# Linear attention in a graph layer: one product for numerators and denominators, divided with nodes on partitions, the quotient turned

## The chip, the cores and the metric

One core of one Trainium2 chip runs the whole program. The metric is the device time of one execution in microseconds. The engines are TensorE (PE, with its weight loads as PEld), VectorE (DVE), ScalarE (ACT), GpSimd (POOL) and SyncE (SP, which only issues transfers here). Each has its own stream of instructions, works it off in order, and waits for the others by semaphores.

## The reference

A layer over 6250 nodes of 256 features: layer norm, then the sum of a graph attention over 100000 edges (sorted by source node), a linear attention with feed-forward part, and a mixture of six experts. What this study touches is the linear attention:

```
q_phi = _phi(q); k_phi = _phi(k)                # (1, 6250, 8 heads, 32)
kv = jnp.einsum('blhd,blhe->bhde', k_phi, v)    # 8 heads x 32 x 32
k_sum = k_phi.sum(axis=1)
z = 1.0 / (jnp.einsum('blhd,bhd->blh', q_phi, k_sum) + 1e-06)
out = jnp.einsum('blhd,bhde,blh->blhe', q_phi, kv, z)
out = out.reshape(Bq, Lq, D_MODEL) @ Wo + bo
x = _layernorm(x + out, ln1_g, ln1_b)
```

## The kernel before, in words

The nodes are worked on in 25 chunks of 250 (two tiles of R = 125 nodes). For each chunk `c` the attention has ten or so steps on three engines. They have no time of their own: they are laid between the steps of another job, the sorting of the edges into tiles. That job is one long sequence of **slots**. Each engine runs through all slots in order, and at each slot `s` calls `attend(s)`, which runs the step with offset `d` for the chunk with `s = 6c + d` (`chunk_at`; SLOT = 6, so a new chunk begins every six slots, and a step with offset 11 runs in the slots 5, 11, 17 ... of its engine). The steps and offsets before the change:

- offset 3, PE `q`: queries with features on partitions, 128x250 per half (L1182)
- offset 4, ACT `attend_q`: exp and relu of them (L1045, L1047); offset 6, ACT `prepare` (L1038), DVE `phi` (L744)
- offset 7, PE `numden`: denominators with nodes on partitions, eight columns from `ks8` (L1191), and numerators with features on partitions from the block diagonal `kv_bd` (L1193)
- offset 8, DVE `invert`: add 1e-6 and invert, 125x16 (L749, L751); ACT `numerators`: copy of them to `att` (L1053)
- offset 9, ACT `inverses`: each inverse is written out 32 times to `rec_row` (L1058)
- offset 10, PE `inverses`: four products with the identity bring them to features on partitions (L1200)
- offset 11, DVE `divide`: `att` times the inverses (L756)
- offset 12, PE `o`: output projection and bias (L1211, L1213)
- offset 13, DVE `attend_sum` and the moments (L762, L285, L290); 14, ACT `root` (L296, L298); 15, DVE `attend_norm` (L770); 16, ACT `normal` (L1065)

The slots fall in three stretches. **Slots 0 to 49**: one masked copy of 128x784 on DVE per slot (L795) and one mask on ACT (L1093); PE has nothing but attention. **Slots 50 to 57** lie between small steps on DVE that make tables. **From slot 58** on a pass `k` (30 of them) has four slots. DVE makes in it the one-hot operands of run `k`: `first_half` (L904), slot, `low_half` (L907), slot, `payload` (L910, L911), slot, `join` (L919), slot. PE multiplies in it those of run `k-1`: slot, 7 products (`compact` part 0, L1238), slot, 7, slot, 7, slot, 7. The two are tied:

```
def first_half(k):
    if k >= 2:
        dve.wait_ge(gathered_up, k - 1)
...
    if part == 0:
        pe.wait_ge(spread_out, k + 1)
```

So DVE can't begin pass `k` before PE has ended pass `k-1`, and in pass `k` PE needs what DVE made in pass `k-1`. Slot 58 is 10 modulo 12; the attention's slots therefore fall on the passes in a pattern of three passes, which take two chunks: slots 10, 11, 0, 1 (modulo 12) in the first kind of pass, 2, 3, 4, 5 in the second, 6, 7, 8, 9 in the third.

Of the kernel before, what the change touches and what calls it, by code (L numbers as in the profile page):

```python
# [13 lines left out]
F32 = mybir.dt.float32  # L14
# [9 lines left out]
R = 125  # L24
# [103 lines left out]
def gps_kernel(nc, x, src, dst, gW, gWb, ga, gab, Wq, bq, Wk, bk, Wv, bv, Wo, bo, W1, b1, W2, b2,  # L128
# [7 lines left out]
    with ExitStack() as ctx:  # L136
# [6 lines left out]
        bank = [ctx.enter_context(nc.psum_tensor(f"bank{i}", [128, 512], F32)) for i in range(8)]  # L143
# [69 lines left out]
        kv_bd = take(2, 128)  # L213
        ks8 = take(2, 8)
# [10 lines left out]
        rec_row = take(2, 8, HD)  # L225
# [113 lines left out]
        QB, HEADS, NUM, DEN, OUT = 1, 2, 3, 4, 5  # L339
# [53 lines left out]
        m_inv = sem("m_inv")  # L393
# [47 lines left out]
        with nc.Block() as block:  # L441
# [128 lines left out]
            def _(dve):  # L570
# [162 lines left out]
                step(V.memset(ks8, 0.0))  # L733
                for h in range(2):
                    V.tensor_tensor(kv_bd[:, h, :], bank[KV + h][:, 0:128], diag_mask, ALU.mult)
                    last_i = V.tensor_scalar(ks8[:, h, 4 * h:4 * h + 4], diag_mask.rearrange("p (h e) -> p h e", h=4)[:, :, 0],
                                             bank[KV + h][:, 128:129], None, ALU.mult)
# [8 lines left out]
                def invert(c):  # L746
                    dve.wait_ge(m_nd, at(c, 1, 1))
                    wait(dve, m_rec, at(c))
                    V.tensor_scalar(den8[0:R, :, :], bank[HEADS][0:R, 0:16].rearrange("p (r h) -> p r h", r=2), 1e-6, None, ALU.add).then_inc(m_den, 1)  # L749
                    dve.wait_ge(m_den, at(c, 2, 1))  # L750
                    V.reciprocal(rec8[0:R, :, :], den8[0:R, :, :]).then_inc(m_den, 1)  # L751

                def divide(c):
                    dve.wait_ge(m_rec, at(c, 1, 1))
                    dve.wait_ge(m_num, at(c, 1, 1))
                    V.tensor_tensor(att, att, bank[DEN][:, 0:2 * CH].rearrange("p (m n) -> p m n", m=2), ALU.mult).then_inc(m_att, 1)  # L756
# [15 lines left out]
                def attend(slot):  # L772

                    c = chunk_at(slot, 15)
                    if c is not None:
                        attend_norm(c)
                    c = chunk_at(slot, 13)
                    if c is not None:
                        attend_sum(c, at(c) % 2)
                    c = chunk_at(slot, 11)  # L780
                    if c is not None:
                        divide(c)
                    c = chunk_at(slot, 8)
                    if c is not None:
                        invert(c)
                    c = chunk_at(slot, 6)
                    if c is not None:
                        phi(c)
# [166 lines left out]
            def _(act):  # L955
# [112 lines left out]
                def attend(slot):  # L1068

                    c = chunk_at(slot, 16)  # L1070
                    if c is not None:
                        normal(c, at(c) % 2)
                    c = chunk_at(slot, 14)
# [3 lines left out]
                    if c is not None:  # L1077
                        inverses(c)
                    c = chunk_at(slot, 8)
                    if c is not None:  # L1080
                        numerators(c)
# [31 lines left out]
            def _(pe):  # L1113
# [72 lines left out]
                def numden(c):  # L1186
                    pe.wait_ge(m_phi, at(c, 1, 1))
                    wait(pe, m_att, at(c))
                    for r in range(2):
                        for m in range(2):  # L1190
                            T.matmul(bank[HEADS][0:R, 8 * r:8 * r + 8], phiq[:, m, r * R:(r + 1) * R], ks8[:, m, :], start=(m == 0), stop=(m == 1))  # L1191
                    for m in range(2):
                        last = T.matmul(bank[NUM][:, m * CH:(m + 1) * CH], kv_bd[:, m, :], phiq[:, m, :], start=True, stop=True)  # L1193
                    last.then_inc(m_nd, 1)

                def inverses(c):
                    pe.wait_ge(m_inv, at(c, 1, 1))
                    for m in range(2):
                        for r in range(2):
                            last = T.matmul(bank[DEN][:, m * CH + r * R:m * CH + (r + 1) * R],  # L1200
                                            rec_row[0:R, r, 4 * m:4 * m + 4, :].rearrange("p h e -> p (h e)"), ident[0:R, 0:R], start=True, stop=True)
                    last.then_inc(m_rec, 1)

                def o(c):
                    if at(c) == 0:
                        pe.wait_ge(consts, 4)
                    pe.wait_ge(m_att, at(c, 1, 1))
# [8 lines left out]
                def attend(slot):  # L1216

                    c = chunk_at(slot, 12)
                    if c is not None:
                        o(c)  # L1220
                    c = chunk_at(slot, 10)
                    if c is not None:
                        inverses(c)
# [1158 lines left out]
```

## Time and profile before

| | |
|---|---|
| median of 3 runs | 2300.26 us (2300.15 to 2304.06) |
| profiled execution | 2298.15 us, its span 2296.4 us |
| busy share of the span | PE 83%, PEld 67%, DVE 74%, ACT 64%, POOL 49% |
| mean granted clock of TensorE | 0.926 of full speed |
| DVE's masked copies (slots 0 to 49) | begin at 329.0 us and 409.3 us |
| passes of four slots | first L904 at 450.5 us, last at 676.5 us |

A span is the time from the first instruction to the last. Busy shares are means over stages with different limits; the attention touched here lives between about 336 and 670 us, and what a step costs has to be read there. In the rows, "idle before" in brackets is how long the engine had stood still, and which engine and line ended the wait. The full clock of TensorE is 2.4 GHz, and a granted clock of 0.50 is 1.2 GHz.

### The profile page before, as it was taken

How to read it: one execution, taken by the hardware profiler on the slowest of the kernel's cores; microseconds unless marked ns; L12 is line 12 of the kernel's file. 1: busy time of each engine (PE TensorE's matmuls, PEld its weight loads, DVE VectorE, ACT ScalarE, POOL GpSimd, SP SyncE). 2: the span in 40 equal slices, each digit the busy share in tenths (PEclk: the TensorE clock that was granted, in tenths of full speed). 3: DMA queues.
4: the chain of work that ended last, by engine and by line, in shares of the span. 5: the costliest groups of instructions: out<-in, count | busy, mean ns of one | idle time of the engine just before them, and what ended most of it. 6: DMA issues, size and time to landing. Idle time of an engine off the chain costs nothing. (4 is left out here: it accounts for less than half of the span.)

```text
span 2296.4 us, 50185 instructions
## 1 busy us (share of the span) xinstructions
PE 1901.7 (83%) x10177; PEld 1538.0 (67%) x10177; DVE 1709.2 (74%) x5357; ACT 1463.3 (64%) x4497; POOL 1119.3 (49%) x1107
## 2 busy tenths in 40 slices
PE   1588858699983999999999999999998572699996
PEld 0345436488872877778777788787787462588885
DVE  7687878878884888898888888988888552255543
ACT  3566739334422888899888898988988660233332
POOL 2000000011125777777777766777774277255554
PEclk9799979699995999999999999999999665799998
DMA  4312201021113444444444444444442543255553
GB/s 137 87 50 59 59 23 50 27 76 46 44 27 83 122 117 119 121 119 120 117 118 121 114 110 115 120 116 118 117 122 71 178 161 132 65 93 91 94 97 54
DMA packets 132951, 218.68 MB, mean 95 GB/s; under 512 B 41572, under 2 KB 87135, under 8 KB 132655
## 3 DMA queue, kind: packets, MB, share of 16 engines
q0 software_dynamic: 61648, 135.33, 24.5%
q1 hardware_dynamic: 66345, 72.68, 10.6%
q10 hardware_dynamic: 4662, 7.46, 1.1%
q8 instruction: 95, 1.56, 0.3%
q14 instruction: 201, 1.65, 0.2%
HBM read 153.08 MB, written 56.42 MB: 91 GB/s over the span
## 5 line engine op out<-in xcount | busy, mean ns | idle before, releaser
L1362 POOL DMA_INDIRECT area<-wh_table,area x812 | 784.2, 966 | 275.5 <-issue 242.3
L1689 PE MATMUL bank<-area 128*126 x2008 | 495.8, 389 | 41.3 <-ACT area L1602 20.8
L1689 PEld LDWEIGHTS bank<-area 128*126 128x126 f32 x2008 | 358.0, 188 | 116.6 <-issue 67.5
L1395 DVE TENSOR_SCALAR area<-iota_row,area 128x126 f32<-128x126 f32 x1004 | 358.9, 365 | 21.2 <-ACT area L1562 15.4
L1595 ACT ACTIVATE area<-iota_row,area 128x126 f32<-128x126 f32 x753 | 292.9, 389 | 0.0
L2180 POOL DMA_INDIRECT out_dram<-area x108 | 169.6, 1571 | 163.4 <-DVE area L2241 146.6
L1609 ACT ACTIVATE area<-area 128x126 f32<-128x126 f32 x753 | 242.8, 386 | 0.5
L1548 ACT ACTIVATE area<-bank 125x512 bf16<-125x512 f32 x251 | 149.0, 594 | 85.4 <-DVE area L1409 82.3
L1470 DVE SCALAR_TENSOR_TENSOR acc_mem<-acc_mem,area,bank 125x258 f32 x251 | 120.6, 480 | 100.3 <-PE bank L1677 84.1
L1709 PE MATMUL bank<-area 128*128 128x250 f32 x800 | 188.6, 379 | 6.2 <-ACT area L1616 3.5
L1665 PE MATMUL bank<-ident,area 128*126 128x128 f32 x1004 | 162.0, 284 | 33.9 <-DVE area L1395 33.8
L1720 PE MATMUL bank<-area 128*125 128x256 f32 x800 | 189.6, 380 | 0.0
L559 POOL IOTA acc_mem<- 50x812 f32 x1 | 0.8, 807 | 353.5 <-DVE area L828 353.5
L1409 DVE TENSOR_REDUCE area<-bank 125x1 f32<-125x512 f32 x251 | 171.4, 683 | 0.0
L1709 PEld LDWEIGHTS bank<-area 128*128 128x128 f32 x800 | 153.1, 192 | 26.6 <-ACT area L1616 3.9
L1720 PEld LDWEIGHTS bank<-area 128*125 128x125 f32 x800 | 150.4, 188 | 23.7
L2241 DVE SCALAR_TENSOR_TENSOR area<-bank,area 128x256 f32<-128x256 f32 x108 | 47.3, 480 | 143.3 <-PE bank L2338 77.4
L564 POOL DMA_INDIRECT sorted_slots<-area x28 | 46.0, 1641 | 216.5 <-DVE area L919 203.4
L2273 ACT ACTIVATE area<-bank,area 128x256 f32<-128x256 f32 x108 | 45.3, 471 | 139.8 <-issue 133.6
L1665 PEld LDWEIGHTS bank<-ident,area 128*126 128x126 f32 x1004 | 106.5, 141 | 39.1 <-DVE area L1395 38.7
L1880 POOL DMA_INDIRECT moe_rows<-area x100 | 99.7, 997 | 66.8 <-ACT area L2030 37.0
L1562 ACT ACTIVATE area<-area,iota_blk 128x4 f32 x251 | 74.8, 298 | 54.8 <-SPq L1354 32.4
(416 smaller groups left out, 4147.8 us busy)
## 6 DMA issues: line engine op xcount, KB each, us to landing
area<-moe_rows SPq DMA_DIRECT2D x54, 264.0 KB, 2.7
area<-wh_table,area POOLq DMA_INDIRECT x812
area<-area SPq DMA_DIRECT2D x18, 388.5 KB
wh_table<-area SPq DMA_DIRECT2D x50, 126.5 KB
xn<-in_x_dram SPq DMA_DIRECT2D x25, 250.0 KB
xt_rows<-area SPq DMA_DIRECT2D x50, 125.0 KB, 2.4
area<-xt_rows SPq DMA_DIRECT2D x25, 250.0 KB, 2.6
x_rows<-area SPq DMA_DIRECT2D x25, 250.0 KB
```

The costliest lines, as they stand in the source:

```text
L1362: g.indirect_dma_start(out=gath[:, (i + GT) % RS, :], out_offset=None, in_=table, in_offset=bass.IndirectOffsetOnAxis(ap=idx_tab[:, i:i + ...
L1395: ins = V.tensor_scalar(xm[:, b, t, :], iota_row[:, :], rowl[:, j % 10, t:t + 1], fetched(j, D)[:, t:t + 1], ALU.is_equal, ALU.mult)
L1409: V.tensor_reduce(gmax[0:R, b:b + 1], bank[XT[j % 2]][0:R, :], AX.X, ALU.max).then_inc(d_m, 1)
L1470: V.scalar_tensor_tensor(row, row, alpha[0:R, j % 5:j % 5 + 1], bank[US[b]][0:R, 0:WROW], ALU.mult, ALU.add).then_inc(d_acc, 1)
L1548: A.activation(hot[0:R, b, :], bank[XT[j % 2]][0:R, :], ACT.Sign).then_inc(a_hot, 1)
L1595: last = A.activation(dist[:, t, :], iota_row[:, :], ACT.Abs, bias=rowl[:, j % 10, t:t + 1], scale=-1.0)
L1609: last = A.activation(sm[:, b, t, :], dist[:, t, :], ACT.Exp, bias=e3[:, b, t:t + 1], scale=-1.0e12)
L1665: last = T.transpose(bank[XT[j % 2]][0:RW, t * L:(t + 1) * L], xm[:, b, t, :], ident[:, :])
L1689: last = T.matmul(bank[US[b]][0:RW, 0:WROW], sm[:, b, t, :], gath[:, bass.ds(place + t, 1), 0:WROW].rearrange("p a w -> p (a w)"), start=( ...
L1709: last = T.matmul(bank[HB[p % 2]][:, i * CH:(i + 1) * CH], w_1[:, k, f * 128:(f + 1) * 128], x1T[:, k, :], start=(k == 0), stop=(k == 1))
L1720: last = T.matmul(bank[AB][0:R, r * D:(r + 1) * D], hT[:, f, r * R:(r + 1) * R], w_2[:, f, :], start=(f == 0), stop=(f == 7))
L2180: g.indirect_dma_start(out=out, out_offset=bass.IndirectOffsetOnAxis(ap=rowi[:, j % RB6, s, MW - 2:MW - 1], axis=0), in_=yo[:, j % 3, s, : ...
```

## The change

Numerators and denominators come from one product. `kvs` holds, for each head, its 32 columns of `kv` and `k_sum` as a 33rd; four products with nodes on partitions (125x132 each) write eight heads of 33 columns for both tiles of the chunk into two neighbouring banks (`twin`). VectorE adds 1e-6 to the 33rd columns and inverts them, and divides right behind, still at offset 8, with the inverse broadcast over 32 columns; the quotient goes to `rows_att`. PE turns it by four transposes at offset 9, ACT copies it to `att` at offset 9, and the projection `o` follows at offset 11. ACT's writing out of the inverses and PE's four products with the identity are gone. The steps behind come one slot earlier: `attend_sum` at 12, `root` at 13, `attend_norm` at 14, `normal` at 15.

```diff
-        bank = [ctx.enter_context(nc.psum_tensor(f"bank{i}", [128, 512], F32)) for i in range(8)]
+        bank = [ctx.enter_context(nc.psum_tensor(f"bank{i}", [128, 512], F32)) for i in range(2)]
+        twin = ctx.enter_context(nc.psum_tensor("twin", [128, 1024], F32))
+        bank += [twin[:, 0:512], twin[:, 512:1024]]
+        bank += [ctx.enter_context(nc.psum_tensor(f"bank{i}", [128, 512], F32)) for i in range(4, 8)]
...
-        QB, HEADS, NUM, DEN, OUT = 1, 2, 3, 4, 5
+        QB, TURN, OUT = 1, 4, 5
+        heads2 = twin[:, :].rearrange("p (r x) -> p r x", r=2)[0:R, :, 0:8 * (HD + 1)].rearrange("p r (h e) -> p r h e", e=HD + 1)
...
                 def invert(c):
                     dve.wait_ge(m_nd, at(c, 1, 1))
-                    wait(dve, m_rec, at(c))
-                    V.tensor_scalar(den8[0:R, :, :], bank[HEADS][0:R, 0:16].rearrange("p (r h) -> p r h", r=2), 1e-6, None, ALU.add).then_inc(m_den, 1)
+                    V.tensor_scalar(den8[0:R, :, :], heads2[:, :, :, HD], 1e-6, None, ALU.add).then_inc(m_den, 1)
                     dve.wait_ge(m_den, at(c, 2, 1))
                     V.reciprocal(rec8[0:R, :, :], den8[0:R, :, :]).then_inc(m_den, 1)
 
                 def divide(c):
-                    dve.wait_ge(m_rec, at(c, 1, 1))
-                    dve.wait_ge(m_num, at(c, 1, 1))
-                    V.tensor_tensor(att, att, bank[DEN][:, 0:2 * CH].rearrange("p (m n) -> p m n", m=2), ALU.mult).then_inc(m_att, 1)
+                    dve.wait_ge(m_den, at(c, 2, 2))
+                    wait(dve, m_rec, at(c))
+                    V.tensor_tensor(rows_att[0:R, :, :, :], heads2[:, :, :, 0:HD], rec8[0:R, :, :].unsqueeze(3).to_broadcast([R, 2, 8, HD]),
+                                    ALU.mult).then_inc(m_att, 1)
...
                 def attend(slot):
 
-                    c = chunk_at(slot, 15)
+                    c = chunk_at(slot, 14)
                     if c is not None:
                         attend_norm(c)
-                    c = chunk_at(slot, 13)
+                    c = chunk_at(slot, 12)
                     if c is not None:
                         attend_sum(c, at(c) % 2)
-                    c = chunk_at(slot, 11)
-                    if c is not None:
-                        divide(c)
                     c = chunk_at(slot, 8)
                     if c is not None:
                         invert(c)
+                        divide(c)
...
-                def numerators(c):
-                    act.wait_ge(m_nd, at(c, 1, 1))
+                def attended_rows(c):
+                    act.wait_ge(m_rec, at(c, 1, 1))
                     wait(act, m_o, at(c))
-                    A.copy(att, bank[NUM][:, 0:2 * CH].rearrange("p (m n) -> p m n", m=2)).then_inc(m_num, 1)
-
-                def inverses(c):
-                    act.wait_ge(m_den, at(c, 2, 2))
-                    wait(act, m_rec, at(c))
-                    A.copy(rec_row[0:R, :, :, :], rec8[0:R, :, :].unsqueeze(3).to_broadcast([R, 2, 8, HD])).then_inc(m_inv, 1)
+                    A.copy(att, bank[TURN][:, 0:2 * CH].rearrange("p (m n) -> p m n", m=2)).then_inc(m_num, 1)
...
                     for r in range(2):
                         for m in range(2):
-                            T.matmul(bank[HEADS][0:R, 8 * r:8 * r + 8], phiq[:, m, r * R:(r + 1) * R], ks8[:, m, :], start=(m == 0), stop=(m == 1))
-                    for m in range(2):
-                        last = T.matmul(bank[NUM][:, m * CH:(m + 1) * CH], kv_bd[:, m, :], phiq[:, m, :], start=True, stop=True)
+                            last = T.matmul(bank[2 + r][0:R, m * 4 * (HD + 1):(m + 1) * 4 * (HD + 1)], phiq[:, m, r * R:(r + 1) * R],
+                                            kvs[:, m, :, :].rearrange("p h e -> p (h e)"), start=True, stop=True)
                     last.then_inc(m_nd, 1)
 
-                def inverses(c):
-                    pe.wait_ge(m_inv, at(c, 1, 1))
+                def turn_rows(c):
+                    pe.wait_ge(m_att, at(c, 1, 1))
+                    wait(pe, m_num, at(c))
                     for m in range(2):
                         for r in range(2):
-                            last = T.matmul(bank[DEN][:, m * CH + r * R:m * CH + (r + 1) * R],
-                                            rec_row[0:R, r, 4 * m:4 * m + 4, :].rearrange("p h e -> p (h e)"), ident[0:R, 0:R], start=True, stop=True)
+                            last = T.transpose(bank[TURN][:, m * CH + r * R:m * CH + (r + 1) * R],
+                                               rows_att[0:R, r, 4 * m:4 * m + 4, :].rearrange("p h e -> p (h e)"), ident[0:R, 0:R])
                     last.then_inc(m_rec, 1)
...
                 def attend(slot):
 
-                    c = chunk_at(slot, 12)
+                    c = chunk_at(slot, 11)
                     if c is not None:
                         o(c)
-                    c = chunk_at(slot, 10)
+                    c = chunk_at(slot, 9)
                     if c is not None:
-                        inverses(c)
+                        turn_rows(c)
                     c = chunk_at(slot, 7)
                     if c is not None:
                         numden(c)
```

How the order of instructions moves is shown at two places, with the kernel's own semaphores in brackets (those that the row waits for).

The first is DVE in the second and third kind of pass, which begin with the row of `first_half`, L904. Before the change: L749 and L751 are `invert`, L770 the norm, L756 `divide`, L744 `phi`, L762 the sum.

```order
L904 TENSOR_TENSOR area<-acc_mem 128x7x424 [waits gathered_up]
L749 TENSOR_SCALAR area<-bank 125x16 [waits m_rec,m_nd]
L751 RECIPROCAL area<-area 125x16 [waits m_den]
...
L756 TENSOR_TENSOR area<-area,bank 128x500 [waits m_num,m_rec]
L904 TENSOR_TENSOR area<-acc_mem 128x7x424 [waits gathered_up]
L744 SCALAR_TENSOR_TENSOR area<-area 128x500 [waits m_qa]
L907 TENSOR_TENSOR area<-acc_mem,area 128x1792
L762 TENSOR_TENSOR area<-bank,area 125x512 [waits m_xs,m_n,m_o,rank_step]
```

After it, with the new kernel's lines (L772 the norm, L750 and L752 `invert`, L757 `divide`, L764 the sum, L287 and L292 the moments, L746 `phi`):

```order
L904 TENSOR_TENSOR area<-acc_mem 128x7x424 [waits gathered_up]
L772 SCALAR_TENSOR_TENSOR area<-area 125x2 [waits m_n,m_rs0,m_va0]
L750 TENSOR_SCALAR area<-twin 125x16 [waits m_nd]
L752 RECIPROCAL area<-area 125x16 [waits m_den]
L757 TENSOR_TENSOR area<-twin,area 125x512 [waits m_rec,m_den]
...
L904 TENSOR_TENSOR area<-acc_mem 128x7x424 [waits gathered_up]
L764 TENSOR_TENSOR area<-bank,area 125x512 [waits m_n,m_xs,m_o]
L287 BN_STATS area<-area 125x6 [waits m_ln0]
...
L292 BN_AGGR area<-area 125x2 [waits m_ln0]
...
L746 SCALAR_TENSOR_TENSOR area<-area 128x500 [waits m_qa]
```

The division has moved from the end of the second kind of pass to its first slot, behind `first_half`; in the third kind the sum and the moments now stand ahead of `phi`.

The second place is PE from the start of the second kind of pass to that of the third. L1238 (before) and L1230 (after) are the products of `compact`. Before:

```order
L1238 MATMUL bank<-area 128x128 [waits staged,spread_out]
L1238 MATMUL bank<-area 128x128 x6
L1182 MATMUL bank<-area 128x250 [waits m_qa,m_xc]
L1182 MATMUL bank<-area 128x250 x3
L1238 MATMUL bank<-area 128x128 x7
L1200 MATMUL bank<-ident,area 128x125 [waits m_inv]
L1200 MATMUL bank<-ident,area 128x125 x3
L1238 MATMUL bank<-area 128x128 x14
L1211 MATMUL bank<-area 125x256 [waits m_ln0,m_att]
```

After (L1192 turns the quotient, L1174 is `q`, L1203 and L1205 are `o`, L1183 is `numden`):

```order
L1230 MATMUL bank<-area 128x128 [waits staged,spread_out]
L1230 MATMUL bank<-area 128x128 x6
L1192 MATMUL bank<-ident,area 128x125 [waits m_num,m_att]
L1192 MATMUL bank<-ident,area 128x125 x3
L1174 MATMUL bank<-area 128x250 [waits m_qa,m_xc]
L1174 MATMUL bank<-area 128x250 x3
L1230 MATMUL bank<-area 128x128 x14
...
L1230 MATMUL bank<-area 128x128 x7
L1230 MATMUL bank<-area 128x128 [waits staged,spread_out]
L1230 MATMUL bank<-area 128x128 x6
L1183 MATMUL twin<-area 125x132 [waits m_att,m_phi]
```

The turn, which waits for the division (m_att), now stands behind the first seven products of its pass, with `q` and the rest of the pass behind it; in the next pass `numden`, which waits for `phi`, stands behind the first seven products, where the projection stood ahead of them before.

## Rows read from the trace of the kernel before

**Rows 1.** Windows: us, busy of PE, PEld, DVE, ACT, POOL (instructions), granted clock, DMA.

```profile
385.00:410.00 25.00, 19.25 (x99) 14.47 (x97) 23.41 (x40) 24.57 (x47) 0.00 (x0) 1.00 0.21 59
545.00:650.00 105.00, 100.33 (x670) 85.88 (x668) 88.22 (x146) 45.31 (x115) 18.69 (x12) 1.00 0.18 44
```

**Rows 2.** Timeline of DVE over three passes: start us, us, line, operation.

```profile
558.42 1.71 DVE L904 TENSOR_TENSOR area<-acc_mem 128x2968 f16<-128x2968 f16 x1 [1.92 <-PE bank L1238]
560.04 1.09 DVE L907 TENSOR_TENSOR area<-acc_mem,area 128x1792 f16<-128x1792 f16 x1
561.16 0.68 DVE L756 TENSOR_TENSOR area<-area,bank 128x500 f32<-128x500 f32 x1
561.76 1.09 DVE L910 TENSOR_TENSOR area<-area,acc_mem 128x1792 f16<-128x1792 f16 x1
...
563.88 0.68 DVE L744 SCALAR_TENSOR_TENSOR area<-area 128x500 f32<-128x500 f32 x1
...
568.12 1.71 DVE L904 TENSOR_TENSOR area<-acc_mem 128x2968 f16<-128x2968 f16 x1 [1.62 <-PE bank L1238]
569.74 0.17 DVE L749 TENSOR_SCALAR area<-bank 125x16 f32<-125x16 f32 x1
569.94 0.25 DVE L751 RECIPROCAL area<-area 125x16 f32<-125x16 f32 x1
...
574.10 1.70 DVE L904 TENSOR_TENSOR area<-acc_mem 128x2968 f16<-128x2968 f16 x1
...
577.42 0.69 DVE L762 TENSOR_TENSOR area<-bank,area 125x512 f32<-125x512 f32 x1
...
579.21 1.06 DVE L910 TENSOR_TENSOR area<-area,acc_mem 128x1792 f16<-128x1792 f16 x1
...
583.84 1.71 DVE L904 TENSOR_TENSOR area<-acc_mem 128x2968 f16<-128x2968 f16 x1 [1.93 <-PE bank L1238]
```

**Rows 3.** Timeline of PE over the same passes.

```profile
561.89 1.13 PE L1211 MATMUL bank<-area 128*125 128x256 f32 x4 [0.95 <-DVE area L756]
...
564.52 1.00 PE L1238 MATMUL bank<-area 128*128 128x128 f16 x7
565.34 0.95 PE L1191 MATMUL bank<-area 128*125 128x8 f32 x8
...
567.08 1.83 PE L1238 MATMUL bank<-area 128*128 128x128 f16 x14
568.74 1.87 PE L1182 MATMUL bank<-area 128*128 128x250 f32 x8
570.44 1.00 PE L1238 MATMUL bank<-area 128*128 128x128 f16 x7
571.26 1.07 PE L1200 MATMUL bank<-ident,area 125*128 125x125 f32 x8
572.17 1.84 PE L1238 MATMUL bank<-area 128*128 128x128 f16 x14
```

**Rows 4.** Timeline of PE in the graph part: four transposes and what follows them.

```profile
806.92 0.59 PE L1698 MATMUL bank<-ident,area 125*128 125x125 f32 x4
807.35 0.24 PE L1677 MATMUL bank<-own_mem,area 125*128 x4
```

**Rows 5.** Windows around a fall of the clock, columns as in rows 1.

```profile
506.00:508.00 2.00, 1.05 (x9) 0.75 (x7) 1.97 (x4) 2.00 (x5) 0.00 (x0) 1.00 0.32 60
508.00:512.00 4.00, 4.00 (x10) 2.38 (x10) 2.67 (x4) 0.04 (x1) 0.99 (x1) 0.57 0.11 36
```

**Rows 6.** Timeline of PE in slots 50 to 57, clock at 0.50.

```profile
420.73 2.07 PE L1211 MATMUL bank<-area 128*125 128x256 f32 x4 [2.74 <-DVE area L756]
...
425.52 1.64 PE L1191 MATMUL bank<-area 128*125 128x8 f32 x7
```

**Rows 7.** Lines L795 and L1058: count, ns min/median/max, first and last start.

```profile
L795 DVE COPY_PREDICATED acc_mem<-acc_mem,area x50: 969/1037/1075, 329.0 to 409.3; 128x784 f32<-128x784 int32 x50
...
L1058 ACT COPY area<-area x25: 600/618/627, 342.6 to 658.0; 125x512 f32<-125x512 f32 x25
```

More of the change, by code:

```diff
@@ L212, in gps_kernel @@
         bias_q = take(2)
-        kv_bd = take(2, 128)
-        ks8 = take(2, 8)
+        kvs = take(2, 4, HD + 1)
         den8, rec8 = take(2, 8), take(2, 8)
@@ L224, in gps_kernel @@
         xs = take(3, 2, D)
-        rec_row = take(2, 8, HD)
+        rows_att = take(2, 8, HD)
         attended = take.place[0]
@@ L392, in gps_kernel @@
         m_rec = sem("m_rec")
-        m_inv = sem("m_inv")
         m_num = sem("m_num")
@@ L732, in _ @@
                 dve.wait_ge(p_kvd, NT)
-                step(V.memset(ks8, 0.0))
                 for h in range(2):
-                    V.tensor_tensor(kv_bd[:, h, :], bank[KV + h][:, 0:128], diag_mask, ALU.mult)
-                    last_i = V.tensor_scalar(ks8[:, h, 4 * h:4 * h + 4], diag_mask.rearrange("p (h e) -> p h e", h=4)[:, :, 0],
+                    V.tensor_tensor(kvs[:, h, :, 0:HD], bank[KV + h][:, 0:128].rearrange("p (h e) -> p h e", h=4),
+                                    diag_mask.rearrange("p (h e) -> p h e", h=4), ALU.mult)
+                    last_i = V.tensor_scalar(kvs[:, h, :, HD], diag_mask.rearrange("p (h e) -> p h e", h=4)[:, :, 0],
                                              bank[KV + h][:, 128:129], None, ALU.mult)
@@ L1068, in attend @@
                 def attend(slot):
-                    c = chunk_at(slot, 16)
+                    c = chunk_at(slot, 15)
                     if c is not None:
                         normal(c, at(c) % 2)
-                    c = chunk_at(slot, 14)
+                    c = chunk_at(slot, 13)
                     if c is not None:
@@ L1077, in attend @@
                     if c is not None:
-                        inverses(c)
-                    c = chunk_at(slot, 8)
-                    if c is not None:
-                        numerators(c)
+                        attended_rows(c)
                     c = chunk_at(slot, 6)
@@ L1206, in o @@
                         pe.wait_ge(consts, 4)
-                    pe.wait_ge(m_att, at(c, 1, 1))
+                    pe.wait_ge(m_num, at(c, 1, 1))
                     wait(pe, m_ln[0], at(c, 2, -1))
@@ L1216, in attend @@
                 def attend(slot):
-                    c = chunk_at(slot, 12)
+                    c = chunk_at(slot, 11)
                     if c is not None:
                         o(c)
-                    c = chunk_at(slot, 10)
+                    c = chunk_at(slot, 9)
                     if c is not None:
-                        inverses(c)
+                        turn_rows(c)
                     c = chunk_at(slot, 7)
```

## The prediction

> **What bounds the kernel now.** I began with the windows of the two long stretches in which the attention runs [rows 1]. In slots 0 to 49 ScalarE is busy 24.6 of 25 us and VectorE 23.4, TensorE only 19.3: the masks and copies set the pace, some 9.7 us per chunk (50 slots begin within 80.3 us, with a slow start) [rows 7]. From slot 58 on it is TensorE: 100.3 of 105 us busy, VectorE 88.2, ScalarE 45.3 [rows 1]. The timelines show how these two are tied. VectorE begins each pass (L904) only when TensorE has ended the pass before: it waits 1.92, 1.62 and 1.93 us for L1238 [rows 2]. TensorE goes from pass to pass without a break: its 14 products at 567.08 span the border, which lies after the seventh, at 567.08 + 1.66 / 2 = 567.91, and VectorE starts at 568.12. So **both start a pass at the same moment, VectorE 0.21 us later**. Three passes, two chunks, take 583.84 - 558.42 = 25.4 us.
>
> The same timeline shows the danger. In the first kind of pass TensorE comes to the projection and waits for the division, which stands behind 1.62 + 1.12 us of VectorE's own work: 0.95 us idle, and the product starts at 561.89, 0.05 us after the division ends (561.16 + 0.68) [rows 2, 3]. Nothing behind it on TensorE goes ahead. That is the only wait of length in a set.
>
> **The work that goes and comes.** TensorE, from start to start [rows 3]: `numden` 1.74 us (565.34 to 567.08), the products with the identity 0.91 (571.26 to 572.17), `q` 1.70, seven products 0.82, the projection 2.63. The new `numden` is four products, each of two passes through the array as L1191's and L1200's are, 132 columns each; L1200's eight of 125 columns take 0.91, so 0.91 is my value, between 0.81 (L1191, eight columns) and 1.74. Four transposes of the very shape take 0.43 us in the graph part [rows 4]; at worst 0.91, as now. So TensorE saves 0.83 + 0.48 = 1.3 us per chunk. ScalarE loses one of two copies, 0.62 us [rows 7]. VectorE keeps its instructions; the new division reads 125x512 out of two banks with a broadcast inverse, which no row shows. It is nearest to L762 (125x512, one operand in a bank), 0.69 us; at worst twice that, were the pattern to halve the rate. The division now waits for the reciprocal just ahead of it, so I give `invert` 0.5 us instead of its 0.20 + 0.17 [rows 2]. The setup of `kvs` against `kv_bd` and `ks8` happens once and is worth nothing here.
>
> **The waits that come.** I lay the new order over the same durations, time counted from TensorE's start of a pass; VectorE starts at 0.21 and adds 0.05 to release TensorE.
>
> *First kind* (slots 10, 11, 0, 1). TensorE: 7 products, projection, 14 products: done at 0.82 + 2.63 + 1.66 = 5.1. Then `numden` needs `phi`, which now stands behind the sum: 1.62 + 1.12 + 2.12 (561.76 to 563.88), sum and moments 1.79 (577.42 to 579.21), `phi` 0.68 [rows 2], 7.33 in all, on TensorE 7.6. Pause 2.5. With 0.91 + 0.82 the pass ends at 9.3.
>
> *Second kind* (2 to 5). After 0.82 TensorE needs the quotient: VectorE does `first_half` 1.62, the norm 0.13 (my estimate from L749's 0.17), `invert` 0.5, `divide` 0.69, that is 2.94, on TensorE 3.2. Pause 2.4, and `q`, 14 products of the pass, the projection and 7 more stand behind it: 0.43 + 1.70 + 1.66 + 2.63 + 0.82 = 7.2. End at 10.4. ScalarE's copy lies under `q`.
>
> *Third kind* (6 to 9). After 0.82 `numden` needs `phi` behind the sum: 1.62 + 1.79 + 0.68 + 0.26 = 4.35, pause 3.5; then 0.91 + 1.66, to 6.9. The turn needs the division in the third slot: 1.62 + 1.79 + 0.60 + 1.12 + 2.12 + 0.13 + 0.5 + 0.69 + 0.26 = 8.8, pause 1.9. Then 0.43 + 1.70 + 0.82: 11.8.
>
> Together 31.5 us against 25.4. The first pass may look shorter than today's 9.7, but the two others go from 6.0 and 9.7 to 10.4 and 11.8. The chunks fill passes 1 to 24, that is 8 sets: **+49 us** at full clock. The 1.3 us saved per chunk is in this sum already. It shortens TensorE where it then waits.
>
> **The clock.** The row of a fall: in 506 to 508 TensorE was busy 1.05 of 2 us, and from 508 to 512 the granted clock is 0.57 of full, while 4 us of work stood waiting [rows 5]. That was one pause of about a microsecond in dense work; many like it do nothing (clock 1.00 over 545 to 650) [rows 1]. The new set has four pauses of 2 to 3.5 us. At the 1.2 GHz level the projection takes 4.79 us (420.73 to 425.52) against 2.63 [rows 3, 6], 2.16 more. I expect two such losses per set, one behind the first two pauses and one behind the next two (part of a third falls into the pause that follows it): 2 x 2.16 x 8 = **+35 us**; bounds 0 and 8 per set, +64.
>
> The Trainium skill's page "TensorE: Matmul & The Clock Gate", Part 4 (PE-mode transpose), adds that the full clock does not engage for transposes, which are not counted as busy like products. It speaks against this change, since the first thing behind the long pause is now a transpose; no row here separates the two, and by it the low stretches would last longer, toward the upper bound.
>
> **Slots 0 to 49.** After the division come turn, `q` and projection on TensorE, 0.43 + 1.70 + 2.63 and some 0.25 for hand-overs, 5.0 us, before the sum four slots later, which four copies of about 1.04 us cover by 4.1 [rows 7]. So VectorE waits 0.9 per chunk at full clock, where ScalarE's lost copy gives back about 0.6: +0.5 net, and some 4.5 if TensorE is at 1.2 GHz there. Six chunks: +3 to +27, taken as **+12**. Slots 50 to 57, where TensorE is at 1.2 GHz already, **+2**.
>
> Sum: 49 + 35 + 12 + 2 = +98 us on the profiled execution of 2298.15, 2396; the median of the runs is 2.1 us above that execution, less than I can resolve.
>
> **The rivals.**
> - *A: as above, waits and lost clock*, 2396, from 2370 to 2440. Chance 0.60.
> - *B: the waits come, the clock holds.* For it speaks that TensorE in slots 0 to 49 is busy 19.3 of 25 us at clock 1.00 [rows 1]. 49 + 3 + 1: 2351. With a slower division (0.69 more in the two passes whose turn waits, 1.4 per set) it is 2362. Chance 0.22.
> - *C: the clock stays at 1.2 GHz through most of it.* All of TensorE's work between waits at 1.83 times its length (4.79 / 2.63) makes a set about 45 us: +157, with +27 before it 2480. Against it: with work so long TensorE hardly pauses, and the clock comes back as it did at 512. Chance 0.05.
> - *D: the other side, faster.* If VectorE ran ahead of TensorE, each quotient would be ready when asked for, and TensorE's saving would count: 16 chunks x 1.3 = 21 us, and ScalarE's copy 0.6 x 6 = 4: 2273. It decides at a lead of 3.5 us at the start of a pass; L904's waits show a lead of -0.21 in all three passes, held there by `gathered_up`. Chance 0.08. The skill's same page, Part 3 (The mechanism), says that products keep program order and only weight loads are pulled ahead; that excludes that `q` or the sort's products slip past the waiting turn, and the wait of 0.95 us agrees.
> - *E: no change*, waits and saving cancel. A set at full clock would have to have 4.2 us of pauses (25.4 less 21.2 of work), not the 10.3 above. Chance 0.04.
>
> The range reaches from B to the top of A, 2345 to 2440, and holds 0.8. A measurement of this kernel can tell about 0.2% from no change. Slower by over 0.2%: A, B and C and a rest, 0.89; faster 0.08; within 0.03.
>
> **What would show it.** L904 of neighbouring passes should lie about 9, 10.5 and 12 us apart at full clock, more where it falls, and no longer 9.7, 6.0, 9.7. The transposes should be listed as waiting for the division and L1183 for `phi`, 2 to 3.5 us each time. TensorE should lose 8 passes per chunk from its busy time and yet have a mean clock under 0.926. L904 should wait for TensorE 3 us and more in the second kind of pass. The stretches behind the sort (graph, experts) should be as now. I am wrong if the transposes don't wait, or if `phi` is early; the size is wrong if the clock stays at 1.00 in the passes, or if the new division takes much over 0.7 us.

## The result, and the profile after

The changed kernel takes 2376.44 us (median of four runs, 2371.96 to 2380.22) against 2300.2; the ratio is 1.033, 95% interval 1.031 to 1.035. It is slower, as forecast, by 76 us where 96 were forecast. The profiled execution took 2371.96 us with this span:

```profile
span 2370.2 us, 49727 instructions
```

The first question is where the 73.8 us of span lie. Three starts divide it: the masked copies of slots 0 to 49 (L795), the first one-hot pass (L904), the last. The rows give a line's count, ns min/median/max, and its first and last start. After the change:

```profile
L795 DVE COPY_PREDICATED acc_mem<-acc_mem,area x50: 1024/1040/1066, 328.0 to 428.9; 128x784 f32<-128x784 int32 x50
...
L904 DVE TENSOR_TENSOR area<-acc_mem x28: 1632/1705/1708, 470.4 to 758.9; 128x2968 f16<-128x2968 f16 x28
```

The row of L904 before is the partner of the second:

```profile
L904 DVE TENSOR_TENSOR area<-acc_mem x28: 1633/1704/1765, 450.5 to 676.5; 128x2968 f16<-128x2968 f16 x28
```

| stretch, us | before | forecast | after | difference |
|---|---|---|---|---|
| ahead of the first L795 | 329.0 | 0 | 328.0 | -1.0 |
| slots 0 to 49 (L795, [rows 7]) | 80.3 | +12 | 100.9 | +20.6 |
| last L795 to first L904 | 41.2 | +2 | 41.5 | +0.3 |
| passes (first to last L904) | 226.0 | +84 | 288.5 | +62.5 |
| behind the last L904 | 1619.9 | 0 | 1611.3 | -8.6 |

What answers to [rows 2] is VectorE's timeline over three passes, one of each kind; the first, second and third kind begin at 572.03, 582.36 and 594.29:

```profile
572.03 1.71 DVE L904 TENSOR_TENSOR area<-acc_mem 128x2968 f16<-128x2968 f16 x1 [3.14 <-PE bank L1230]
...
576.90 0.69 DVE L764 TENSOR_TENSOR area<-bank,area 125x512 f32<-125x512 f32 x1
...
578.69 0.65 DVE L746 SCALAR_TENSOR_TENSOR area<-area 128x500 f32<-128x500 f32 x1
...
582.36 1.70 DVE L904 TENSOR_TENSOR area<-acc_mem 128x2968 f16<-128x2968 f16 x1 [2.89 <-PE bank L1230]
...
584.54 0.69 DVE L757 TENSOR_TENSOR area<-twin,area 125x512 f32<-125x512 f32 x1
...
594.29 1.71 DVE L904 TENSOR_TENSOR area<-acc_mem 128x2968 f16<-128x2968 f16 x1 [5.68 <-PE bank L1230]
595.91 0.69 DVE L764 TENSOR_TENSOR area<-bank,area 125x512 f32<-125x512 f32 x1
...
597.70 0.65 DVE L746 SCALAR_TENSOR_TENSOR area<-area 128x500 f32<-128x500 f32 x1
...
602.08 0.69 DVE L757 TENSOR_TENSOR area<-twin,area 125x512 f32<-125x512 f32 x1
...
606.04 1.71 DVE L904 TENSOR_TENSOR area<-acc_mem 128x2968 f16<-128x2968 f16 x1 [3.15 <-PE bank L1230]
```

And to [rows 3], TensorE:

```profile
579.39 2.12 PE L1183 MATMUL twin<-area 128*125 128x132 f32 x8 [2.36 <-DVE area L746]
581.31 1.85 PE L1230 MATMUL bank<-area 128*128 128x128 f16 x14
585.29 1.09 PE L1192 MATMUL bank<-ident,area 125*128 125x125 f32 x4 [2.13 <-DVE area L757]
586.18 3.04 PE L1174 MATMUL bank<-area 128*128 128x250 f32 x8
...
598.40 1.77 PE L1183 MATMUL twin<-area 128*125 128x132 f32 x8 [3.31 <-DVE area L746]
...
602.83 0.65 PE L1192 MATMUL bank<-ident,area 125*128 125x125 f32 x4 [1.00 <-DVE area L757]
603.31 1.85 PE L1174 MATMUL bank<-area 128*128 128x250 f32 x8
```

The reader is to see four waits of TensorE in three passes, each ended by VectorE, on the two instructions that the forecast named: `numden` (L1183) for `phi` (L746), 2.36 and 3.31 us, and the turn (L1192) for the division (L757), 2.13 and 1.00. Each time the instruction waited for ends just before: 597.70 + 0.65 = 598.35, and L1183 starts at 598.40. VectorE in turn waits for TensorE at each L904, and longest, 5.68 us, behind the second kind of pass, where the turn, `q` and the projection stand behind the wait. The passes last 10.3, 11.9 and 11.75 us, a set (three passes, two chunks) 34.0. Over all passes VectorE's waits at L904 for TensorE grew from 25.0 to 92.5 us, and the passes grew by 62.5.

Added up between 340 and 740 us, in the view of the waits (us in total, times, longest):

```profile
DVE area L904 <- PE bank L1230: 90.0, 22, 5.8
...
PE twin L1183 <- DVE area L746: 70.5, 24, 7.2
...
PE bank L1192 <- DVE area L757: 43.7, 24, 6.7
...
DVE area L764 <- PE bank L1205: 23.8, 8, 3.4
```

Of the last line, the sum's wait for the projection, 21.1 us lie before 431 us, in slots 0 to 49. The 7.2 and 6.7 us are single waits at the start of the passes and in slots 50 to 57; inside the passes that follow, the waits have the lengths shown above.

### The profile page after: what moved, and what is told of

Its sections match the earlier page's. It is cut to its first block and busy times, and to the rows that moved or that the text cites. A ratio compares the mean times of both kernels' runs of the same rounds, so it can differ in the third digit from the quotient of the medians.

```text
span 2370.2 us, 49727 instructions
## 1 busy us (share of the span) xinstructions
PE 1909.9 (81%) x9977; PEld 1540.5 (65%) x9977; DVE 1712.2 (72%) x5356; ACT 1457.1 (61%) x4472; POOL 1118.3 (47%) x1107
## 5 line engine op out<-in xcount | busy, mean ns | idle before, releaser
L1387 DVE TENSOR_SCALAR area<-iota_row,area 128x126 f32<-128x126 f32 x1004 | 359.9, 366 | 23.1 <-ACT area L1554 18.4
L1681 PE MATMUL bank<-area 128*126 x1008 | 249.3, 390 | 17.8 <-ACT area L1601 14.0
L1681 PE MATMUL twin<-area 128*126 x1000 | 248.0, 391 | 16.6 <-ACT area L1594 13.9
L1681 PEld LDWEIGHTS bank<-area 128*126 128x126 f32 x1008 | 180.1, 188 | 54.7 <-issue 29.2
L1681 PEld LDWEIGHTS twin<-area 128*126 128x126 f32 x1000 | 179.2, 189 | 54.1 <-issue 29.3
L904 DVE TENSOR_TENSOR area<-acc_mem 128x2968 f16<-128x2968 f16 x28 | 47.7, 1702 | 92.5 <-PE bank L1230 92.5
L1230 PE MATMUL bank<-area 128*128 128x128 f16 x784 | 102.6, 299 | 5.0 <-DVE area L919 5.0
L1183 PE MATMUL twin<-area 128*125 128x132 f32 x200 | 46.4, 402 | 74.0 <-DVE area L746 74.0
L1540 ACT ACTIVATE area<-bank 125x512 bf16<-125x512 f32 x126 | 74.7, 593 | 50.2 <-DVE area L1401 49.3
```

The lines of the kernel that those rows point to most:

```text
L1230: last = T.matmul(bank[KV + k % 2][:, 0:2 * LO], oh_hi[k % 2][:, c // WI, :, c % WI], vl[k % 2][:, c // WI, :, :, c % WI].rearrange("p v l ...
L1387: ins = V.tensor_scalar(xm[:, b, t, :], iota_row[:, :], rowl[:, j % 10, t:t + 1], fetched(j, D)[:, t:t + 1], ALU.is_equal, ALU.mult)
L1681: last = T.matmul(bank[US[b]][0:RW, 0:WROW], sm[:, b, t, :], gath[:, bass.ds(place + t, 1), 0:WROW].rearrange("p a w -> p (a w)"), start=( ...
```

## The experiments

**The new products in the old order.** The decisive experiment: if the order makes the waits, the same products with the old distances between steps must be faster than the kernel before. The diffs of this part are against the changed kernel, unless another is named. ScalarE's copy goes to 10 too, root, norm and normal to 14, 15 and 16.

```diff
-                    c = chunk_at(slot, 11)
+                    c = chunk_at(slot, 12)
                     if c is not None:
                         o(c)
-                    c = chunk_at(slot, 9)
+                    c = chunk_at(slot, 10)
                     if c is not None:
                         turn_rows(c)
...
-                    c = chunk_at(slot, 12)
+                    c = chunk_at(slot, 13)
                     if c is not None:
                         attend_sum(c, at(c) % 2)
```

> The changed kernel's products and division, with the steps behind the division put back: turn and ScalarE's copy at offset 10, projection at 12, sum at 13, root 14, norm 15, normal 16. Theory (the order makes the waits): in the first kind of pass phi is early again (TensorE 7.6 us, one short pause), in the second the quotient is ready when the turn comes (VectorE binds, 6.4), in the third VectorE binds with 8.75; a set of three passes takes 22.7 us at full clock against 34.0 in the changed kernel and 25.4 before. Passes 28 x some 7.6 us, slots 0 to 49 about 78 us, whole about 2278 us, faster than before by 0.9%. Rival (the new products, the division out of two banks or the transposes are themselves dear, or the clock stays low because of transposes): a set stays at 28 us or more and the time at 2330 or more.

Measured: 2275.96 us (2270.38 to 2279.88), ratio 0.9914 to the kernel before, interval 0.9884 to 0.9943. VectorE's timeline has a third, a first and a second kind of pass here:

```profile
560.16 1.70 DVE L904 TENSOR_TENSOR area<-acc_mem 128x2968 f16<-128x2968 f16 x1
568.67 1.70 DVE L904 TENSOR_TENSOR area<-acc_mem 128x2968 f16<-128x2968 f16 x1
576.40 1.67 DVE L904 TENSOR_TENSOR area<-acc_mem 128x2968 f16<-128x2968 f16 x1
582.54 1.70 DVE L904 TENSOR_TENSOR area<-acc_mem 128x2968 f16<-128x2968 f16 x1
```

8.51, 7.73 and 6.14 us, where 8.75, 7.6 and 6.4 were worked out, and no idle time ahead of L904: VectorE binds now. Together they make 22.4, where the expectation had 22.7. The price of the new product shows at full clock on TensorE:

```profile
563.09 1.08 PE L1183 MATMUL twin<-area 128*125 128x132 f32 x8
564.00 1.84 PE L1230 MATMUL bank<-area 128*128 128x128 f16 x14
```

0.91 us for `numden`, the forecast's value, against 1.74 before [rows 3]. The new products are cheap and the order alone turned their gain into a loss. Two numbers of the expectation were missed, and they work against each other. The passes took 198.6 us, 27.4 less than before, where 2.7 less for each of eight sets makes 22. And slots 0 to 49 took 86.2 us, not 78. The waits there (336 to 412 us) say why:

```profile
PE bank L1203 <- ACT area L1053: 16.2, 7, 2.7
...
DVE area L764 <- PE bank L1205: 7.4, 5, 1.9
```

The projection waited for ScalarE's copy of the turned quotient, which stands behind `normal` in their common slot (1.08 us in the timeline).

**ScalarE's copy ahead of normal.** The kernel in the old order again (the last one), with ScalarE's two steps exchanged:

```diff
+                    c = chunk_at(slot, 10)
+                    if c is not None:
+                        attended_rows(c)
                     c = chunk_at(slot, 16)
                     if c is not None:
                         normal(c, at(c) % 2)
```

> The late order with one exchange on ScalarE: at their common slot its copy of the turned quotient stands ahead of normal, not behind it. In the late kernel's slots 0 to 49 TensorE waited 2.0 to 2.7 us per chunk for that copy, with the projection and the sum behind it and a clock of 0.77. Theory: the wait falls below 1 us, VectorE's wait for the projection goes, slots 0 to 49 fall from 86 to about 80, whole about 2270 us. Rival (ScalarE's normal, now later, holds the norm chain or the stores, or the clock stays low anyway): no change, 2276.

Measured: 2267.5 us (2265.68 to 2271.34), ratio to the kernel before 0.9874, interval 0.9853 to 0.9895. This still overlaps the interval of the last kernel; the gain over that one is read from the profiles. Slots 0 to 49 fell from 86.2 to 78.3 us. The wait for the copy only shrank from 16.2 to 11.5 us in sum (same stretch), not below 1 us each as expected (it is still 1.8 us), but VectorE no longer waits for the projection:

```profile
PE bank L1203 <- ACT area L1053: 11.5, 7, 1.8
```

**The turn alone a slot later.**

```diff
-                    c = chunk_at(slot, 9)
+                    c = chunk_at(slot, 10)
                     if c is not None:
                         turn_rows(c)
...
-                    c = chunk_at(slot, 9)
+                    c = chunk_at(slot, 10)
                     if c is not None:
                         attended_rows(c)
```

> The changed kernel with only the turn and ScalarE's copy behind it moved from offset 9 to 10; sum still ahead of phi. Theory: the wait of TensorE for the division goes (2.4 us in the second kind of pass, 1.9 in the third), the waits of numden for phi stay (2.5 and 3.5). A set takes 9.3 + 8.4 + 9.4 = 27.1 us at full clock, some 29 with lost clock, against 34.0; whole about 2335 us. Rival (one late phi holds the whole set, so the other wait only moves): set stays at 32 or more, whole over 2360.

Measured: 2323.11 us in one run. The sets take 30.0, 28.8, 29.9, 30.0 and 28.8 us. The waits of TensorE for the division are gone from the longest ones, those for `phi` stay (470 to 720 us; 46.9 us in the changed kernel):

```profile
PE twin L1183 <- DVE area L746: 39.3, 15, 3.4
```

So the wait for the division is worth 53 us of the 76 against the changed kernel, somewhat more than the 41 of the expectation; slots 0 to 49 gave 13.6 of it (100.9 to 87.3), the passes 36.8 (288.5 to 251.7). The lowered clock that goes with the wait is in this sum.

**Phi alone ahead of the sum.**

```diff
                 def attend(slot):
...
+                    c = chunk_at(slot, 6)
+                    if c is not None:
+                        phi(c)
                     c = chunk_at(slot, 12)
                     if c is not None:
                         attend_sum(c, at(c) % 2)
```

> The changed kernel with only phi put ahead of the sum on VectorE within their common slot. Theory: numden's waits shrink by 1.8 us each (2.5 to 0.7, 3.5 to 1.7), but in the third kind of pass the turn still waits for the division at 8.8 us, so that its saving goes into that wait; a set takes 7.6 + 10.4 + 11.8 = 29.8 at full clock, some 32 with lost clock; whole about 2360 us. Rival (phi is the main wait): under 2340.

Measured: 2349.04 us in one run, 27 less than the changed kernel, where 2360 was expected. Three passes, a second, a third and a first kind:

```profile
561.67 1.70 DVE L904 TENSOR_TENSOR area<-acc_mem 128x2968 f16<-128x2968 f16 x1 [0.21 <-PE bank L1230]
573.37 1.71 DVE L904 TENSOR_TENSOR area<-acc_mem 128x2968 f16<-128x2968 f16 x1 [5.44 <-PE bank L1230]
587.18 1.71 DVE L904 TENSOR_TENSOR area<-acc_mem 128x2968 f16<-128x2968 f16 x1 [5.22 <-PE bank L1230]
594.83 1.71 DVE L904 TENSOR_TENSOR area<-acc_mem 128x2968 f16<-128x2968 f16 x1 [0.20 <-PE bank L1230]
```

The first kind of pass falls from 10.3 to 7.65 (587.18 to 594.83), as worked out (7.6); the second stays at 11.7, and the third grows to 13.8 from 11.75. `phi` was early there, but the division was not: the wait moved to the turn (up to 3.3 us in this kernel, against 1.00 in that pass of the changed one), and the clock over 573 to 587 us was 0.79, with turn, `q` and seven products behind the wait. Half of a repair moves a wait. Over the whole stretch some of the gain is left: the passes took 272.0 us, 16.5 less than in the changed kernel.

**The old products in the new order.** The other side of the first experiment: the kernel before, with projection, sum, root, norm and normal one slot earlier.

```diff
-                    c = chunk_at(slot, 12)
+                    c = chunk_at(slot, 11)
                     if c is not None:
                         o(c)
...
-                    c = chunk_at(slot, 13)
+                    c = chunk_at(slot, 12)
                     if c is not None:
                         attend_sum(c, at(c) % 2)
```

> The kernel before, with its old products, its two copies and its division at offset 11, but projection at 11, sum 12, root 13, norm 14, normal 15, as the changed kernel has them. Theory (the order makes the waits, whatever the products): TensorE waits for the division 2.0 and 1.4 us, and numden for a phi that stands behind the sum, 3.5 us in the third kind of pass; a set takes 10.8 + 10.0 + 10.3 = 31 us at full clock against 25.4, with lost clock 33; whole about 2350 to 2370 us. Rival (the new products are what costs): within 10 us of 2300.

Measured: 2404.81 us in one run, outside the 2350 to 2370 expected, on the far side from the rival. TensorE again:

```profile
588.02 1.13 PE L1211 MATMUL bank<-area 128*125 128x256 f32 x4 [1.79 <-DVE area L756]
...
611.07 1.85 PE L1191 MATMUL bank<-area 128*125 128x8 f32 x8 [3.31 <-DVE area L744]
```

The 3.31 us for `phi` is the same as in the changed kernel, with other products behind it. Sets take 35 to 37 us, where 33 with lost clock were expected. The granted clock over 560 to 662.4 us was 0.78, so the kernel lost more by it than the expectation allowed; how much more was not measured. With the first experiment this makes a table of four, medians or single runs: old products 2300 in the old order and 2405 in the new; new products 2276 and 2376. The order costs about 100 us with either; the products save some 20 us in the old order (2276 against the runs of the kernel before made beside it, ratio 0.9914) and 28 in the new. (The old orders of the two are not the same to the step, since the new division stands at offset 8 in both.)

**Filler in the waits.** What does the lowered clock cost? Filler means products whose result nothing reads, put ahead of a wait so that TensorE works in the time in which it would stand idle.

```diff
+                def fill(n):
+                    for _ in range(n):
+                        T.matmul(bank[0][:, 0:128], spin, spin, start=True, stop=True)
                 def numden(c):
+                    fill(14)
                     pe.wait_ge(m_phi, at(c, 1, 1))
...
                 def turn_rows(c):
+                    fill(14)
                     pe.wait_ge(m_att, at(c, 1, 1))
```

> The changed kernel, with 14 products 128x128 of the identity (bf16) into a bank that nothing reads, put on TensorE ahead of numden and 14 ahead of the turn. They take 1.66 us at full clock, less than each of the waits there (1.9 to 3.5 us worked out), so that they delay nothing; they leave the waits but make them short of idle time. Theory (part of the loss is the lowered clock): a set of three passes falls from 34.0 to near the 31.5 us of full clock, slots 0 to 49 from 101 to about 87, the whole to about 2342 us and the mean clock rises over 0.93. Rival (the clock costs nothing on the path, the waits are all): the set stays at 34 and the whole at 2375, or grows by the filler.

Measured: 2343.07 us in one run, 33 less than without the filler. Of the sets some run as worked out for full clock:

```profile
612.79 1.71 DVE L904 TENSOR_TENSOR area<-acc_mem 128x2968 f16<-128x2968 f16 x1 [3.15 <-PE bank L1238]
622.20 1.71 DVE L904 TENSOR_TENSOR area<-acc_mem 128x2968 f16<-128x2968 f16 x1 [1.96 <-PE bank L1238]
632.55 1.71 DVE L904 TENSOR_TENSOR area<-acc_mem 128x2968 f16<-128x2968 f16 x1 [4.09 <-PE bank L1238]
644.29 1.71 DVE L904 TENSOR_TENSOR area<-acc_mem 128x2968 f16<-128x2968 f16 x1 [3.14 <-PE bank L1238]
```

9.41, 10.35 and 11.74 us: the forecast had 9.3, 10.4 and 11.8 for full clock. Others still have a low stretch in the second kind (12.1), which makes 33.3, and the mean clock rose to 0.921, not over 0.93 as expected. All passes together took 273.8 us, 14.7 less than in the changed kernel. Over 350 to 410 us the clock was 1.00, and slots 0 to 49 took 82.5 us, 18.4 less. More work on TensorE made the program faster, since it fell into idle time.

**Transposes or products.** The Trainium skill's page "TensorE: Matmul & The Clock Gate", Part 4 (PE-mode transpose), says that transposes don't engage the full clock. Two kernels ask for it, both from the changed one: the turn as products with the identity (the first piece), and the transposes kept with filler of about the same length right behind them (the second).

```diff
-                            last = T.transpose(bank[TURN][:, m * CH + r * R:m * CH + (r + 1) * R],
+                            last = T.matmul(bank[TURN][:, m * CH + r * R:m * CH + (r + 1) * R],
...
+                    for _ in range(4):
+                        T.matmul(bank[0][:, 0:128], spin, spin, start=True, stop=True)
```

> The changed kernel with the four transposes written as four products with the identity, as before the change (two passes through the array each). Theory: the turn is 0.48 us longer (0.91 against 0.43) behind each wait for the division, on the path: +8 us in the passes, +3 in slots 0 to 49, about 2387 us, and the stretches at 1.2 GHz stay as they are. Rival (it is the transposes that let the clock down or keep it down): the stretches at 1.2 GHz get shorter, the mean clock rises over 0.91 and the time falls below 2370.

> The changed kernel, its transposes kept, with four products of the identity (bf16, 0.47 us) right behind them, into a bank that nothing reads: the turn now keeps TensorE as long as the kernel turn_product does, which had a clock of 0.85 over 560 to 662.4 us against 0.80 in the changed kernel. Theory (it was the longer work, or shorter idle time, that held the clock up, not that products stand in place of transposes): the clock over that stretch is 0.84 or more and a set 34.1. Rival (transposes keep the clock down): it stays at 0.80 and a set rises to 34.5 to 35.

Measured: 2383.68 and 2386.3 us, one run each. The windows of 560 to 662.4 us, three sets of the changed kernel, in the order changed kernel, products, transposes with filler (columns as in rows 1):

```profile
560.00:662.40 102.40, 76.07 (x437) 63.24 (x435) 64.78 (x105) 29.80 (x75) 13.98 (x9) 0.80 0.14 33
```

```profile
560.00:662.40 102.40, 77.09 (x459) 64.93 (x457) 64.77 (x105) 29.87 (x77) 13.99 (x9) 0.85 0.15 33
```

```profile
560.00:662.40 102.40, 76.82 (x459) 64.13 (x459) 64.76 (x105) 29.80 (x75) 13.99 (x9) 0.83 0.15 34
```

Clock 0.80, 0.85, 0.83. The kernel with filler fell between its theory (0.84 or more) and the rival (0.80). The differences depend on the stretch: over 460 to 660 us the three clocks are 0.76, 0.77 and 0.78, so there the order of the last two is turned round. One profile each can't settle so small a difference: no run here bears the Trainium skill's rule out, and none refutes it. What the trace of the changed kernel does show is that transposes run at the full clock where it is granted (0.48 us for four at 602.83, 0.89 at 585.29). In time, sets take 34.1 with products as without, though the turn is longer.

> The late order (turn at offset 10, projection 12, sum 13) with products in place of the transposes. Theory: VectorE binds two of the three kinds of pass, so TensorE's extra 0.48 us shows little: set 22.3 to 22.9, whole within 2276 to 2284. Rival (transposes hurt the clock in slots 0 to 49, where it was 0.77 in the late kernel): slots 0 to 49 fall from 86 to 81 and the whole to 2270.

In the late order products for transposes gave 2276.68 us in one run: the first kind of pass took 7.92 us, not 7.64, so a set is 22.6, and the whole the same as with transposes. Slots 0 to 49 took 83.2 us, between the theory's 86 and the rival's 81, so this doesn't decide about the clock either.

**Filler in the best version.** The fastest kernel so far, with ScalarE's copy ahead of `normal`, gets filler ahead of the turn and of the projection for its first eight chunks:

> The late_rows kernel, with 6 filler products (identity, bf16) ahead of the turn and 10 ahead of the projection for chunks 0 to 7 only, where TensorE waits 0.8 and 1.8 us in slots 0 to 49 and the clock is 0.84. Theory: the clock there rises to 0.95 or more, VectorE then binds, slots 0 to 49 fall from 78.3 to about 76, whole about 2265 us against 2267.5. Rival (the filler is itself in the way, since the waits leave no room at the lower clock): 2270 or more.

Measured: 2266.96 us (2263.56 to 2268.19), ratio 0.9867, interval 0.9839 to 0.9895: no difference from the same kernel without filler. The clock rose from 0.83 to 1.00 over 350 to 400 us, but slots 0 to 49 stayed at 78.3 us, where 76 had been expected. There the clock was not on the path: VectorE and ScalarE are busy 45 and 46 of 50 us, as without filler (45 and 45).

```profile
350.00:400.00 50.00, 34.67 (x225) 26.10 (x222) 45.07 (x80) 46.25 (x85) 0.00 (x0) 1.00 0.18 48
```

**The kernel before once more.**

> The kernel before, unchanged, for a second profile. From the first gather of the graph part to the last it took 1046.4 us in the first profile, 1040.2 in the changed kernel, which touches nothing there. Theory (run to run scatter): this profile shows 1040 to 1046, and 226 us from the first L904 to the last as before. Rival (the change shortened the graph part by 6 us): 1046 again.

Measured: span 2297.4 us, again 226.0 us of passes, and the graph part's gathers from 707.4 to 1750.7 us, 1043.3 against 1046.4 in the first profile:

```profile
L1362 POOL DMA_INDIRECT area<-wh_table,area x812: 942/946/1522, 707.4 to 1750.7; - x163
```

Over all profiles of this study the gathers took 1040 to 1046 us, in kernels of either layout. The changed kernel's 1040.2 (790.2 to 1830.4) is at the low end of that. From the last L904 to the end the twelve other profiles took 1614 to 1622 us, and the two kernels that differ from the changed one only at the turn took 1620.0 and 1622.1. So I put the -8.6 us behind the last pass down to scatter; the kernels that keep the change don't show it.

## Why the prediction was right, and where its sizes were off

**What binds, and the tie of the passes: right.** VectorE starts a pass when TensorE ends the one before, TensorE starts it at the same moment, so a step that one needs from the other in the same pass is always late by VectorE's own work ahead of it. All that was forecast comes from this.

**The prices of the operations: right.** `numden` 0.91 us (forecast 0.91), the turn 0.48 at full clock (602.83 to 603.31; 0.43), the division 0.69 (0.69, so two banks and a broadcast cost nothing), norm, inverse and division 1.25 us from 583.98 to the end at 585.23 (1.32).

**The waits at full clock: right for a set, too large in the sum.** 9.3, 10.4 and 11.8 forecast, 9.41, 10.35 and 11.74 measured with filler. The sum took 6.1 us more for each of eight sets, 49 us. But all passes of the kernel with filler took 273.8 us, 47.8 more than before, and four of its second passes still have a low stretch of some 1.7 us or more. Without these and a low stretch in one first pass it would be about 39 more (my estimate, from the lengths of its passes). The forecast had compared with a set of 25.4 us throughout. Three of the first four sets of the kernel before took 28.5, 27.0 and 27.0, and the first pass of all, which the forecast left out, is 3 us shorter with the new products in either order (10.1 us in both kernels with the old products, 7.1 to 7.2 with the new).

**The clock: mechanism right, size too large.** The forecast took two losses of 2.16 us per set, 35 us in all. With 34.0 per set against 31.5 the loss is 2.5, 20 us in eight sets. The filler took 14.7 us off the passes and did not remove every low stretch, so the clock is worth 15 to some 23 of the 62.5 us, and the waits 39 to 48. This term of the sum was the one most mis-sized. The low stretches do come as forecast (clock 0.80 over three sets). But what runs in them is `numden`, 1.92 us instead of 0.91 (579.39 to 581.31), and the turn, 0.89 (585.29 to 586.18), with `q`, 2.87 for 1.70 (586.18 to 589.05), not the whole projection that I had taken as the measure; and in the third kind of pass the low stretch only eats the wait that follows it: its turn waits 1.00 us, not the 1.9 of full clock, and the pass lasts 11.75 as at full clock.

**Slots 0 to 49: right in kind, too small.** +20.6 us against +12, within the bounds of 3 to 27. The forecast counted six chunks there; seven have their sum in these slots (offset 12, slots 12 to 48), and the view of the waits has seven. The filler's 82.5 us says that 18.4 of it came by the clock, where at full clock the waits cost 2.2 more than before. Here it is the other way round: the lowered clock is nearly all, since TensorE's chain of turn, `q` and projection stands behind a wait, much of it at 1.2 GHz (clock 0.67 over 340 to 410 us), and the sum waits for it.

**Slots 50 to 57: +0.3 for +2.** No step of weight.

In the passes the forecast was 21.5 us too high, in slots 0 to 49 it was 8.6 too low; the stretch behind the passes was 8.6 shorter by scatter, and small stretches gave 2.7 less. Together this makes 74 us of span for 98. That the miss is no larger than that is partly luck. Rival D (faster) needed a lead of VectorE, which is not there. What it would give, 2273, is near the 2276 of the late order, where the quotient is nearly always ready when asked for; but the parts differ, since the passes there fell by 27.4 us and slots 0 to 49 grew by 5.9. The cause named for the direction is shown by undoing it: the order back, 2276; the order alone on the old products, 2405.

## What to carry to other kernels

When two engines start each round of a loop together, write down for each cross-engine request where in its round it is asked for and where it is answered; a step that is moved one place earlier can ask two microseconds before its answer, and everything behind it on its engine waits too. A cheaper computation should be tried with the old distances first; here the same products gave +3.3% or -1.3% of time by the order alone. Look also at what two steps in one slot do to each other on the third engine: the order of two calls on ScalarE was worth 8 us of slots 0 to 49 (86.2 and 78.3, one profile each).

## What I had not expected of the hardware

Filler products in TensorE's waits took 33 us off the changed kernel, 18 of them in the slots 0 to 49, and the same trick was worth nothing in the best version, though the clock rose from 0.83 to 1.00 there: a granted clock is a cost only where TensorE's work is on the path. Eight f32 passes of 132 columns take 0.91 us, where the eight of 8 columns in L1191 took 0.81 [rows 3], so the sixteen-fold product was nearly free; that is why one product for numerators and denominators halves `numden`.
